# A 16-tile attention and gene-mixing kernel: another order of the opening, and another end of the last tile

## The reference

```
xn = layernorm(x)                        # x: 16 x 128 x 512
q = rope(xn @ Wq, pos); k, v = split(ctx @ Wkv); k = rope(k, pos)     # 32 heads of 16
x = x + softmax(q k^T / 4) v @ Wout + bout
y = rmsnorm(layernorm(x)) * norm_w
logits = y @ Wc^T / max(temperature, 0.1)            # 1024 genes
w = softmax over the 32 largest logits of a row, 0 elsewhere
e = w @ genes                                        # 64 columns
x = x + tanh(e @ Wd^T) * y * (e @ Wu^T) * scale
```

## Time and profile before

| what | value |
|---|---|
| median of 3 runs | 516.35 us (513.47 to 518.47) |
| profiled execution | 516.95 us |
| its span in the trace | 515.0 us |
| around the span | 1.95 us |
| busy PE, DVE, ACT, POOL | 441.8, 410.0, 279.4, 261.1 us |
| mean granted TensorE clock | 0.963 of full |
| instructions | 11003 |

### The profile page before, as it was taken

The page is one execution under the profiler, slowest core; times in us unless marked ns, Lnnn a source line. Parts: engine busy times, 40 slices in busy tenths (PEclk is TensorE's granted clock), DMA queues, the critical chain, the costliest instruction groups (busy, mean ns, idle before and its releaser), DMA issues. The chain is left out here.

```text
span 515.0 us, 11003 instructions
## 1 busy us (share of the span) xinstructions
PE 441.8 (86%) x3829; PEld 280.2 (54%) x3829; DVE 410.0 (80%) x661; ACT 279.4 (54%) x424; POOL 261.1 (51%) x262
## 2 busy tenths in 40 slices
PE   3546776978999899899999999999989899888795
PEld 3232554545556566465656565656556565565353
DVE  5781874497989898798888888888898988875993
ACT  3431838264655656465656565657475757354122
POOL 4423718173556556484838393939392929111110
PEclk9956889989999999999999999999999999989999
DMA  5893231725172626244343434343434342310101
GB/s 195 264 198 91 50 74 39 118 23 114 33 124 53 123 55 106 71 76 98 71 102 68 101 69 102 71 103 71 102 74 83 71 86 44 83 23 20 41 1 43
DMA packets 115665, 42.93 MB, mean 83 GB/s; under 512 B 107040, under 2 KB 109104, under 8 KB 115632
## 3 DMA queue, kind: packets, MB, share of 16 engines
q1 hardware_dynamic: 114624, 41.45, 37.8%
q10 hardware_dynamic: 1008, 1.05, 0.6%
HBM read 12.86 MB, written 4.19 MB: 33 GB/s over the span
## 5 line engine op out<-in xcount | busy, mean ns | idle before, releaser
L1229 PE MATMUL gene<-wcT_h,yT 128*128 128x512 f16 x256 | 81.9, 382 | 1.4 <-DMA yT<-y_hl 1.4
L1031 DVE MAX8 top<-stage_b 128x8 f32<-128x1024 f32 x64 | 78.4, 1225 | 3.6
L1039 DVE MATCH_REPLACE8 stage_b<-top,stage_b 128x1024 f32<-128x1024 f32 x64 | 77.5, 1211 | 0.2
L432 POOL TENSOR_TENSOR x_hl<-xn,x_hl 128x512 f16<-128x512 f32 x16 | 18.8, 1175 | 80.3 <-issue 40.7
L472 POOL TENSOR_TENSOR rstd<-var,minus_half 128x1 f32<-128x1 f32 x16 | 8.8, 548 | 93.1 <-DVE var L1003 86.6
L1229 PE MATMUL dense<-wq_h,xT 128*128 128x512 f16 x128 | 43.1, 397 | 7.0 <-DMA xT<-x_hl 4.9
L1229 PE MATMUL gene<-wcT_l,yT 128*128 128x512 f16 x128 | 48.8, 381 | 0.0
L443 POOL TENSOR_TENSOR stage_b<-stage_b,cos_t 128x512 f32<-128x512 f32 x31 | 39.5, 1275 | 15.4 <-issue 11.0
L669 ACT ACTIVATE stage_b<-gene 128x512 f32<-128x512 f32 x32 | 18.8, 590 | 47.8 <-PE gene L1229 47.6
L964 DVE TENSOR_REDUCE row_max<-score_a 128x8 f32<-128x1024 f32 x32 | 39.0, 1219 | 6.5 <-PE score_a L1296 6.2
L444 POOL TENSOR_TENSOR stage_b<-stage_b,sin_t 128x512 f32<-128x512 f32 x31 | 43.6, 1406 | 0.0
(11 more groups left out here) (163 smaller groups left out, 1065.1 us busy)
## 6 DMA issues: line engine op xcount, KB each, us to landing
x_ring<-x_dram SPq DMA_DIRECT2D x16, 256.0 KB, 3.0
out_dram<-x_ring SPq DMA_DIRECT2D x16, 256.0 KB, 2.1
ctx_sb<-ctx_dram SPq DMA_DIRECT2D x16, 128.0 KB, 2.1
wc_raw<-L_ffn_Wc_dram SPq DMA_DIRECT2D x4, 512.0 KB, 6.8
stage_b<-L_xattn_Wq_dram ACTq DMA_DIRECT2D x4, 256.0 KB, 5.2
stage_a<-L_xattn_Wkv_dram SPq DMA_DIRECT2D x2, 512.0 KB, 8.0
stage_a<-L_xattn_Wout_dram SPq DMA_DIRECT2D x1, 1024.0 KB, 9.5
genes_sb<-L_ffn_genes_dram SPq DMA_DIRECT2D x2, 256.0 KB, 4.6
```

The costliest lines, as they stand in the source:

```text
L1031: nc.vector.max(top[:, 8 * n:8 * n + 8], logit if n == 0 else rest).then_inc(s_top[n], 1)
L1039: nc.vector.match_replace(rest, top[:, 8 * n:8 * n + 8], logit if n == 0 else rest, REMOVED).then_inc(s_rem[n], 1)
L1229: last = nc.tensor.matmul(out, lhs(k), rhs(k), start=(n == 0), stop=(n == steps - 1))
```

## The change

The opening. SP and ACT each load a half of tile 0's x. DVE rotates k and q of tile 0, and splits both (`rope0_products`, `rope0_sums`, `split0_lo`, `wk_lo(0)`); POOL does none of that any more. SP issues `turn_x(1)` after bout and x of tile 2, ahead of the Wd, Wu and genes loads and of x of tile 3. PE does `project_q(1)` before `project_k(1)` and `transpose_max(0)`, no longer after them. `spread(WC)` goes ahead of `scoresT(0, 0)`, `wout_lo` ahead of `code_scale`, `wout_hi` to the place before `neg_max_hi(0)`. Jobs 2 and 3 follow directly on `transpose_o(0)`, and each later pair moves up one place, so that iteration 5 holds one pair and not two. `keep_warm` is 9 + 9 + 8 transpositions, in place of 14.

The end. y of tile 15 is transposed on PE (`last_transpose_y`) and split from PSUM, with no DMA. ACT does `norm2_apply(15)` ahead of `read_wT(13)`, and DVE takes `last_y_lo(15)` after the first `remove_top(14)`, not ahead of the search. `combine(14)` moves from the middle of tile 15's search to behind its mask. The mask of tile 15 is done in two halves (`last_mask`), so that the first half can be transposed while the second is masked; `express(15)` starts on its first half. The up part is multiplied by y and the sum's reciprocal (`last_gate`) without tanh, and `last_combine` then multiplies by tanh. Logits of tile 15 go to `score_a`, its transposed weights to `dense`. Numbers of `keep_busy` differ.

```
-            load_x(0)
+            sp.dma_start(slot(0)[0:64], x[0, 0:64]).then_inc(s_x, 16)
...
                 if first(t3):
+                    load_bout()
+                    next_x(2)
+                    turn_x(1)
                     load_late()
-                    next_x(2)
...
-                if later(t2):
+                if later(t2) and not (isinstance(t2, int) and t2 == 1):
                     turn_x(t2)
...
-            wk_lo(0)
-            rope(0, 1)
-            rope_sum(0, 1)
-            split_lo(0, 1)
             ln1(1)
             run(pool, 8, iteration)
...
+            act.dma_start(slot(0)[64:P], x[0, 64:P]).then_inc(s_x_half, 16)
...
+            def last_y_hi(t):
+
+                act.wait_ge(s_last_yT, 1)
+                act.wait_ge(s_lg[0], t)
+                act.wait_ge(s_lg[1], t)
+                nc.scalar.activation(yT[:, 0:DIM], dense[:, 0:DIM], ACT.Copy).then_inc(s_y_h, 1)
...
+                if last_tile(t5):
+                    norm2_apply(t5)
                 if t7 is not None:
                     read_wT(t7, 0)
+                if last_tile(t5):
+                    last_y_hi(t5)
...
+                if first(t4):
+                    wout_hi()
...
+            def last_mask(t):
+                dve.wait_ge(s_rem[3], t + 1)
+                dve.wait_ge(s_gexp, t + 1)
+                halves = [slice(n * 512, (n + 1) * 512) for n in range(2)]
+                for n, done in enumerate((s_gw_first, s_gw)):
+                    nc.vector.scalar_tensor_tensor(gene_w[:, halves[n]], rest[:, halves[n]], REMOVED, gene_w[:, halves[n]],
+                                                   ALU.is_equal, ALU.mult,
+                                                   accum_out=(first_sum, gene_sum)[n][:]).then_inc(done, 1)
...
+            def last_combine(t):
                 dve.wait_ge(s_tanh, t + 1)
-                nc.vector.tensor_tensor(down[:], down[:], yn_of(t), ALU.mult).then_inc(s_t1, 1)
+                dve.wait_ge(s_t1, t + 1)
+                nc.vector.tensor_tensor(down[:], down[:], xn[:], ALU.mult).then_inc(s_t2, 1)
...
+                wout_lo()
                 code_scale()
-                wout_lo()
                 scale_up()
...
+            wk_lo(0)
             wk_lo(1)
             q_scale()
-            for k in range(XK):
+            wq_lo(0)
+            rope0_products(1)
+            for k in (1, 2, 3):
                 wq_lo(k)
+            rope0_sums(1)
+            rope0_products(0)
+            rope0_sums(0)
+            split0_lo(1)
             wv_lo(0)
-            rope_q0()
+            split0_lo(0)
+            wv_lo(1)
             norm1_stats(1)
-            q0_lo()
-            wv_lo(1)
...
+                if last_tile(t7):
+                    last_mask(t7)
+                    combine(TILES - 2)
+                    last_sum(t7)
...
-                if last_tile(t5):
-                    y_lo(t5)
                 if t6 is not None:
                     find_top(t6, 0)
                     remove_top(t6, 0)
+                if last_tile(t5):
+                    last_y_lo(t5)
+                if t6 is not None:
                     find_top(t6, 1)
...
+            keep_warm(9)
             transpose_ctx(0)
-            keep_warm(14)
+            keep_warm(9)
...
             spread(NORM)
+            keep_warm(8)
...
-                if later(t3):
+                if later(t3) and not (isinstance(t3, int) and t3 == 1):
                     project_q(t3)
...
+                    down_up(t7, 1)
+                    down_up(t7, 0)
...
+                if first(t3):
+                    project_q(1)
```

More of the change, by code:

```diff
@@ L376, in iteration @@
                     next_ctx(t1)
-                if t4 is not None:
+                if t4 is not None and not last_tile(t4):
                     turn_y(t4)
@@ L712, in iteration @@
                     read_k(t3)
-                if t5 is not None:
+                if t5 is not None and not last_tile(t5):
                     norm2_apply(t5)
@@ L730, in iteration @@
                     exp_group(t4, 3)
-                if isinstance(t4, int) and t4 == 1:
-                    job_hi(8)
-                    job_hi(9)
-                if t4 is not None:
                     read_oT(t4, 0)
@@ L739, in iteration @@
                     job_hi(1)
+                    job_hi(2)
+                    job_hi(3)
                 if t7 is not None:
@@ L779, in _ @@
             read_v(0)
-            wout_hi()
             run(act, 8, iteration)
@@ L1159, in iteration @@
                     y_lo(t5)
-                if first(t5):
-                    job_lo(8)
-                    job_lo(9)
                 if t7 is not None:
@@ L1168, in iteration @@
                     remove_top(t6, 2)
+                if first(t4):
+                    job_lo(0)
+                    job_lo(1)
                 if t4 is not None:
@@ L1171, in iteration @@
                 if first(t4):
-                    job_lo(0)
-                    job_lo(1)
+                    job_lo(2)
+                    job_lo(3)
+                if t7 is not None and not (isinstance(t7, int) and t7 >= TILES - 2):
+                    combine(t7)
                 if last_tile(t7):
                     last_gate(t7)
-                if t7 is not None:
-                    combine(t7)
-                if last_tile(t7):
+                    last_combine(t7)
                     last_finish(t7)
@@ L1424, in iteration @@
                     transpose_max(t4)
-                if later(t3):
+                if first(t4):
+                    spread(WC)
+                if later(t3) and not (isinstance(t3, int) and t3 == 1):
                     project_q(t3)
@@ L1442, in iteration @@
                     express(t7)
+                if last_tile(t5):
+                    logits(t5, 0)
                 if t4 is not None:
@@ L1464, in iteration @@
                     transpose_job(1)
-                if t7 is not None:
+                if t7 is not None and not last_tile(t7):
                     down_up(t7, 1)
-                if isinstance(t7, int) and t7 == TILES - 3:
-                    keep_busy(6)
+                if last_tile(t5):
+                    logits(t5, 1)
                 if t4 is not None:
                     transpose_o(t4)
-                if t5 is not None:
+                if first(t4):
+                    transpose_job(2)
+                    transpose_job(3)
+                if t5 is not None and not last_tile(t5):
                     logits(t5, 0)
```

181 lines of the change are left out of this document (108 added, 73 removed).

## The result

| | before | changed |
|---|---|---|
| median | 516.75 us (18 runs, 513.47 to 520.65) | 512.69 us (18 runs, 510.79 to 516.36) |
| profiled execution, its span | 516.95, 515.0 us | 510.79, 508.8 us |
| mean granted clock | 0.963 | 0.953 |

The ratio is 0.9931, with a 95% interval from 0.9904 to 0.9959: 0.7% faster, where 1.9% was forecast, and 0.7 us above the range. The profiled execution is the fastest of its 18, so the two traces flatter the change by some 2 us.

What follows compares the result with a forecast made beforehand. Opening bound by a chain of waits, steady part by PE (26 us a tile, unchanged), drain by DVE. 516.95 - 4.9 (opening) - 4.8 (drain) = 507.2 us profiled, 506.7 median, 1.9% less; range 501.5 to 512.

Steps and rivals of the forecast that it cites:

- The drain: Last tiles, from about 470 us, where DVE is the chain: 4.8 us gained, bounds 1.5 and 6.
- behind the mask: Drain, from tile 15's mask to the end: 1.5 us gained, between 0 and 2.3.
- The transposition of x 1 and the hole: Opening: issued earlier on SP, xT usable at 37.0, PE hardly waits; transposed scores of tile 0 at 45.9, gain 4.6 us.
- What then is late: Opening, after tile 0's transposed scores: four jobs eat about 2 us; scores of tile 1 at 64.2, first maximum at 65.0.
- So 4.2 goes on: Opening: the next iteration hangs on tile 1's first maximum, so its 4.2 us gain carries on.
- The moves of wout_lo and wout_hi, and the idle transpositions: Opening: wout_lo counted as 2.78 us on DVE, wout_hi no longer ahead of norm1_apply(1); no cost term in the sum.
- The 0.7 us from one pair less in iteration 5: Iteration 5: one pair of jobs less on ACT before read_oT(1) gains 0.7 us, between 0 and 2.
- PE's order, the rotations and the halves at 0: Opening: x in halves and rotations on DVE cost 0, between -1 and +1 us; PE's order had no separate net cost.
- B: Rival, 25%: the opening's gain is given back in iteration 4, only 2 us of it left, 509.6 us.
- A: Rival, 12%: the clock stays up in the opening, so project_q(1) starts at full clock, 504 us.
- C: Rival, 10%: the drain's PE runs at the low clock, 3 us back, 509.8 us.
- D: Rival, 4%: slower, as xT lands late and all of tile 0 waits behind project_q(1) on PE.

Runs made afterwards that it cites:

- e1: The kernel before with the edits of the end alone, nothing of the opening: 512.65 us, ratio 0.9913.
- e5: e1 plus SP's order only (bout, x 2 and the transposition of tile 1's x ahead of the late loads): 507.45 us, ratio 0.9793.
- e16: The same kernel as e5, measured again: 508.87 us, ratio 0.9862.
- e6: The changed kernel with the five pairs of jobs back in the places of the kernel before: 510.61 us, ratio 0.9858.
- e9: e6 with x 0 in one load on SP's queue: 511.17 us, ratio 0.9904.
- e3: The changed kernel with idle matmuls where PE waits in the first two iterations that have a softmax: 513.10 us, ratio 0.9915.
- e13: e5 with each pair of jobs moved one place earlier: 510.38 us, ratio 0.9891.
- e2: The kernel before with the changed opening only, the old end kept: 518.09 us, ratio 1.0025.
- e17: e5 with PE's new order and both rotations of tile 0 on DVE: 507.76 us, ratio 0.9810.
- e15: The changed kernel as it is, measured again: 511.91 us, ratio 0.9916.
- e14: e5 with, on DVE, y 0's low part ahead of the low parts of jobs 6 and 7, and wout_lo ahead of code_scale: 504.07 us, ratio 0.9765.
- e18: e5 with only wout_lo moved ahead of code_scale on DVE: 505.36 us, ratio 0.9762.

## Why the prediction was right and wrong

*The drain* was right in mechanism and size: 4.8 us forecast, 4.8 in the traces, 4.5 by e1's ratio; 1.46 of it behind the mask (1.5 forecast).

*The transposition of x 1 and the hole* were right: the kernel of e5 and e16 measures 4.5 us for that edit alone, and the transposed scores came at 46.54 in the changed kernel (45.9 forecast).

*"What then is late" is the step that failed.* It put the scores of tile 1 at 64.2 and the first maximum at 65.0; they came at 67.02 and 68.12. From the transposed scores of tile 0 it gave 18.3 us, with the four jobs eating "about 2 us of the 6 or more which ACT gained"; the changed kernel's two traces have 20.5 and 19.8, and e6 and e9, the same opening with the jobs in their old places (e9 also with x 0 in one load), 16.8 each. So the four jobs cost 3.0 to 3.7 us there and not 2, in part by the low clock, since e3 has 18.7. ACT's split of q moved with the jobs (e13 against e16), and in the time the move costs 1.5 to 2.2 us. The forecast also had jobs 0 and 1 begin at 51.9; they began at 54.71, behind value products that waited for ACT's exponentials, but e6 begins them at 55.26 and still has the scores at 64.37. "So 4.2 goes on" failed too: of the 0.5 us left at the scores nothing is found in the time, where the opening brings nothing (changed against e1) or costs 1.3 us (e2).

*The moves of wout_lo and wout_hi, and the idle transpositions,* were given no cost in the sum: 2.78 us were taken for `wout_lo` on DVE, without asking who runs beside it. e9 against e17 gives 3.4 us for the three edits together in the medians. How that divides, and by which wait it reaches the end, stays open: `wout_hi`, `wout_lo` with PE's new order and `keep_warm` were not tried alone, and ACT's 1.8 us for POOL does not show at the scores of tile 1.

The steps from run to run are -4.5 us for SP's order (e1's 512.65 to 508.2), -0.4 for PE's order and rotations (e17), +3.4 for the output weights and `keep_warm` (e9), -0.6 for the halves (e6), +1.9 for the jobs (changed, 512.5). That they add up says nothing, as each run is compared with the next one; only the first and the two large positive ones stand clear of the scatter, or nearly so.

*The 0.7 us from one pair less in iteration 5* can't be confirmed, as the scatter there is 4 us. *PE's order, the rotations and the halves at 0* stand within what the times resolve, although the rotations make the first scores about 1 us later, at the far bound of the forecast.

*Rivals.* B was nearest: the gain given back in iteration 4, in part for the reason that it named (the four jobs), but in full and not 3 of 5 us, since a second giver was missing. A did not happen: the clock was 0.50 from 32 to 40 us of the changed kernel's trace, behind the eight idle transpositions, and 0.87 and then 0.50 in e15's, so tile 1's q projection began at the low clock in both. C did not happen: the clock was 1.00 from 468 to 504 us. D did not: x 1 was used at 37.37. A clock rival for iteration 4 was missing from the list; by e3 it would have been a cost of 1 to 2 us on that stretch, not the whole.

## What to carry to other kernels

A lead won early is worth only what the in-order queues behind it let through: after pricing the wait that goes, walk each engine's list to the next meeting point, and take work that "fits in the gain" as a cost on the engine where the chain passes. Try a bundle's parts alone: here one edit of queue order carried the opening, and two riders, the moved jobs and the bundle around the output weights, cancelled it. A filler belongs where its engine waits in the new schedule; price it again when the order around it changes. And compare single traces with care: one kernel's two traces differed by 2.4 us on the very stretch in question, so a claim on it needs several traces of each kind.

## What the runs showed of the hardware

VectorE and GpSimd can hold each other up for a whole instruction. POOL's 128x512 product takes 1.26 us alone. Beside `wout_lo` it ended 1.12 us after that did: 49.15 against 48.03 in the changed kernel, and in e14, by POOL's and DVE's rows,

```profile
41.91 3.31 POOL L456 TENSOR_TENSOR stage_b<-stage_b,sin_t 128x512 f32<-128x512 f32 x1
```

```profile
41.62 2.48 DVE L903 TENSOR_TENSOR wout_l<-stage_a,wout_h 128x2048 fp32r<-128x2048 f32 x1
```

45.22 against 44.10. Not every operation is held: while the changed kernel's product ran on to 49.15, DVE's operations with a single 128x1 input at 48.26, 48.45 and 48.96 took their usual 0.15 us. It goes the other way too: DVE's 128x1 `shift` of the second norm, with the two inputs `mv` and `rstd` and a median of 0.16 us over its 16 records, took 1.21 us at 76.11 in the changed kernel and ended with POOL's product (76.05 + 1.26 = 77.31). It waits for POOL's `rstd`, behind which POOL goes straight on to a product, so it is caught again at 106.72, 133.52 and 160.88 (1.22 to 1.23 us) and first free at 188.30 (0.16 us), where the product starts after it, at 188.43. The Trainium skill states the rule ("SBUF — State Buffer", section on SBUF's two separate sides) for a VectorE operation in a two-port mode or with two inputs from SBUF, beside a GpSimd operation that reads SBUF: the port pair of the two engines is an exclusive lock for the whole instruction, not a shared bandwidth. The rows agree; applied ahead of the run, it would have put 2 us on one operation of POOL beside `wout_lo`. Whether that costs time is another question: in e18 and e14, the two fastest kernels, the operation takes 3.31 us as well.
